# A Mamba block with a top-2 mixture of experts: the last chunk's output in two parts, and rows added in the result buffer

## The reference, cut to what matters

```python
xz = xn @ W_in                                   # 256 -> 2 x 512
u = silu(causal_conv4(xz[:, :512]) + conv_b)
dt, B, C = split(u @ W_xproj, [16, 32])          # 16, 16, 16
delta = softplus(dt @ W_dt + b_dt)
h[t] = exp(delta[t] * A) * h[t-1] + delta[t] * u[t] * B[t]     # 512 channels x 16 states
y[t] = sum_n h[t] * C[t] + D_skip * u[t]
mamba = (y * silu(z)) @ W_out                    # 512 -> 256
moe = sum over the top 2 of 16 experts: weight * (gelu(ln(xn @ W1 + b1)) @ W2 + b2)
```

## Time and profile before

| | us |
|---|---|
| median of 3 runs | 1177.31 |
| lowest and highest | 1170.78, 1178.3 |
| the profiled execution | 1172.21 |
| its span | 1170.5 |

### The profile page before, as it was taken

How to read it: one execution, slowest core, us unless ns; L and a number is a source line. 1 busy time by engine, 2 the same in 40 slices (tenths; PEclk the granted TensorE clock), 3 DMA queues, 4 the chain that set the end, 5 groups by cost and what they waited for, 6 DMA issues and landing times.

```text
span 1170.5 us, 16709 instructions
## 1 busy us (share of the span) xinstructions
PE 961.2 (82%) x4499; PEld 646.5 (55%) x4499; DVE 1051.2 (90%) x1310; ACT 863.6 (74%) x1787; POOL 839.3 (72%) x549
## 2 busy tenths in 40 slices
PE   5955576697979989789887998899988999778766
PEld 2423244464547656566555756476556665566655
DVE  7699959999999799989688969999899989979993
ACT  3444497655788788867798689978998699967860
POOL 8005488888678677558677786977987768877993
PEclk9966797588979989899998999799997999989886
DMA  9987865763366523834447542763457453854215
GB/s 320 406 355 228 260 199 152 243 231 95 105 223 194 123 65 80 317 101 97 105 118 258 150 101 68 261 205 66 102 151 245 114 121 74 285 167 106 71 18 171
DMA packets 129879, 197.52 MB, mean 169 GB/s; under 512 B 20924, under 2 KB 112744, under 8 KB 121464
## 3 DMA queue, kind: packets, MB, share of 16 engines
q1 hardware_dynamic: 105056, 156.73, 40.1%
q0 software_dynamic: 18288, 22.62, 11.5%
q10 hardware_dynamic: 6440, 17.10, 4.0%
HBM read 150.01 MB, written 54.20 MB: 174 GB/s over the span
## 4 chain that ended last, share of the span: by engine, by line
PE 36%; issue 18%; ACT 15%; DVE 15%; POOL 8%; DMA 3%; ACTq 2%; SPq 1%; POOLq 0%; DVEq 0%
DVE hb L1450 10%; PE psY L1002 7%; POOL hc L613 5%; PE psA L1027 5%; PE psC L1145 4%; ACT hb L774 4%; PE psC L1086 3%; PE psA L1074 3%; DVE psB L1439 3%; ACT hnT L860 2%; PE psE L1122 2%; PE psA L1019 2%; DMA xg<-xs_d 2%; POOL acc_d L653 1%; ACT L863 1%
## 5 line engine op out<-in xcount | busy, mean ns | idle before, releaser
L613 POOL TENSOR_TENSOR hc<-hb,Cb 128x1024 f32<-128x1024 f32 x235 | 597.0, 2612 | 127.3 <-PE psY L1002 70.6
L1450 DVE TENSOR_TENSOR_SCAN hb<-hb,carry,psB 128x512 f32<-128x512 f32 x384 | 471.6, 1264 | 1.4 <-ACT hb L774 1.4
L1002 PE MATMUL psY<-ident,hc 128*128 128x128 f32 x2048 | 315.6, 296 | 74.1 <-POOL hc L613 60.8
L1002 PEld LDWEIGHTS psY<-ident,hc 128*128 128x128 f32 x2048 | 263.6, 153 | 195.6 <-POOL hc L613 90.6
L774 ACT ACTIVATE hb<-delta,aneg 128x512 f32<-128x512 f32 x512 | 349.0, 717 | 15.2 <-DVE delta L1288 7.0
L1439 DVE TENSOR_TENSOR psB<-Bb,psU 128x512 f32<-128x512 f32 x512 | 325.5, 681 | 0.0
L653 POOL DMA_INDIRECT acc_d<-yo,idx x80 | 127.9, 1599 | 67.7 <-DMA acc_d<-yo,idx 23.0
L1450 DVE TENSOR_TENSOR_SCAN hb<-hb,psB 128x512 f32<-128x512 f32 x128 | 149.5, 1204 | 6.1 <-ACT hb L774 6.1
L1027 PE MATMUL psA<-ux,dgw 128*128 128x512 f32 x232 | 120.2, 628 | 11.6 <-ACT ux L718 11.4
L627 POOL DMA_INDIRECT xs_d<-xg,slots x64 | 66.9, 1045 | 50.5 <-issue 27.7
L1145 PE MATMUL psC<-w2r,hnT 128*128 128x256 f32 x320 | 89.1, 426 | 0.0
(11 more groups left out here) (211 smaller groups left out, 1198.1 us busy)
## 6 DMA issues: line engine op xcount, KB each, us to landing
Bb<-bc_d SPq DMA_DIRECT2D x32, 1024.0 KB, 6.4
...
Bb<-in_L_attn_x SPq DMA_DIRECT2D x8, 512.0 KB, 8.9
```

Of the source, the lines that this page charges most:

```text
L613: pool.tensor_tensor(hc[:, k:k + 2, :], hb[:, g % HR:g % HR + 2, :], Cb[:, n:n + 2, :], ALU.mult).then_inc(s_g, 1)
L1002: mm = pe.matmul(y[:, tt * P:(tt + 1) * P], hc[:, g % GR, tt * P:(tt + 1) * P], ident[:, :], start=False, stop=(n == NS - 1), is_transpose ...
L1450: dve.tensor_tensor_scan(h, h, psB[g % 2][:, :], first, ALU.mult, ALU.add).then_inc(s_scan, 1)
```

## The change

- Chunk 7's quarters 0 to 2 are transposed, projected and copied to `om` during the last units (`p_tr`, `p_trc`, `p_mm`, `p_copy`), and GpSimd adds them as an eighth chunk add at unit 509. Gate 2 of chunk 7 moves from unit 62 to 52. Behind the last gate one transpose per tile, two copies of 128 x 256 and four projections are left; VectorE adds them to the rows read back in two additions of 128 x 512, and SyncE stores two halves.
- All adds go to `out`, which now has the padding rows; the copy of 3584 rows is gone, and the host takes the middle 4096 rows.
- Pairs 176, 186, 200 and 414 leave `HC_DVE` and so go to GpSimd.
- `idx` moves by one unit, W1's centring (`CEN0`) by one, and some forty entries of the tables by one to a few units.

```diff
 AT = {
...
-    "gate": [30, 39, 52, 2],
+    "gate": [30, 39, 52, 3],
...
 AT7 = {
...
-    "gate": [37, 40, 63, 2],
+    "gate": [36, 40, 52, 3],
...
+    "p_tr": [53, 56, 57, 59],
+    "p_trc": [56, 58, 60, 60],
+    "p_mm": [53, 58, 59, 63],
+    "p_copy": [57, 59, 60, 60],
 }
...
-HC_DVE = [0, 2, 4, 6, 8, 10, 14, 16, 22, 38, 54, 72, 78, 86, 146, 176, 184, 186, 200, 398, 414]
+HC_DVE = [0, 2, 4, 6, 8, 10, 14, 16, 22, 38, 54, 72, 78, 86, 146, 184, 398]
...
-    "idx": [5],
+    "idx": [6],
...
-CEN0 = 5
+CEN0 = 6
...
-    return tiles + ([("chunk", c - 1, 0)] if c > 0 and s == AT["e_copy"][TT - 1] + 2 else [])
+    if c > 0 and s == AT["e_copy"][TT - 1] + 2:
+        tiles.append(("chunk", c - 1, 0))
+    if c == NC - 1 and s == AT7["p_copy"][TT - 1] + 1:
+        tiles.append(("chunk", c, 0))
+    return tiles
...
+        def dc_out(c):
+
+            return DC - 1 if c == NC - 1 else DC
...
         def acc_rows(c):
-            return acc_d[1 + c * T:1 + (c + 1) * T, :].rearrange("(a p) d -> p a d", p=P)
+            return out[1 + c * T:1 + (c + 1) * T, :].rearrange("(a p) d -> p a d", p=P)
...
             sp.dma_start(yo[:, :, :], acc_rows(NC - 1)).then_inc(s_fa, 16)
-            sp.dma_start(out[0:NT - T, :].rearrange("(p a) d -> p (a d)", p=P),
-                         acc_d[1:1 + NT - T, :].rearrange("(p a) d -> p (a d)", p=P)).then_inc(s_fo, 16)
-            for tt in range(TT):
-                r = (NC - 1) * T + tt * P
-                sp.wait_ge(s_eo, tt + 1)
-                sp.dma_start(out[r:r + P, :], om[:, tt, :]).then_inc(s_fo, 16)
-            sp.wait_ge(s_fo, 16 * (1 + TT))
+            for k in range(2):
+                sp.wait_ge(s_eo, k + 1)
+                sp.dma_start(acc_rows(NC - 1)[:, 2 * k:2 * k + 2, :], om[:, 2 * k:2 * k + 2, :]).then_inc(s_fo, 16)
+            sp.wait_ge(s_fo, 16 * 2)
...
+                    if c == NC - 1:
+                        for tt in range(TT):
+                            for _ in at(c, "p_trc", s, tt, tt + 1):
+                                y_copy(c, tt)
+                            for _ in at(c, "p_copy", s, tt, tt + 1):
+                                o_copy(c, tt)
...
+            act.wait_ge(s_ltm, 1)
+            act.wait_ge(s_eom, NC * TT)
+            for k in range(2):
+                act.activation(ygT[:, 2 * k:2 * k + 2, :], psC[:, 2 * k * P:2 * (k + 1) * P].rearrange("p (a b) -> p a b", a=2),
                                ACT.Copy).then_inc(s_et, 1)
...
+            pe.wait_ge(s_c, len(C_TURN))
             for tt in range(TT):
...
+                mm = pe.matmul(psC[:, tt * P:(tt + 1) * P], zs[:, tt, (DC - 1) * P:DC * P], ident[:, :],
+                               start=True, stop=True, is_transpose=True)
+            mm.then_inc(s_ltm, 1)
...
+            for k in range(2):
+                pe.wait_ge(s_et, k + 1)
+                for a in range(2):
+                    mm = pe.matmul((psE, psA)[k][:, a * D:(a + 1) * D], ygT[:, 2 * k + a, :], wout[:, DC - 1, :],
+                                   start=True, stop=True)
+                mm.then_inc(s_lom, 1)
...
-            for tt in range(TT):
-                dve.wait_ge(s_eom, (NC - 1) * TT + tt + 1)
-                dve.tensor_tensor(om[:, tt, :], (psC, psE)[tt % 2][:, 0:D], yo[:, tt, :], ALU.add).then_inc(s_eo, 1)
+            for k in range(2):
+                dve.wait_ge(s_lom, k + 1)
+                dve.tensor_tensor(om[:, 2 * k:2 * k + 2, :], (psE, psA)[k][:, :].rearrange("p (a d) -> p a d", a=2),
+                                  yo[:, 2 * k:2 * k + 2, :], ALU.add).then_inc(s_eo, 1)
```

More of the change, by code:

```diff
@@ L75 @@
 AT0 = {
-    "x_load": [31],
+    "x_load": [34],
     "x_mm": [7, 7, 11, 12, 12, 13, 18, 18, 21, 21, 22, 23, 26, 29, 32, 32, 33, 33, 33, 34, 36, 36, 37, 37],
-    "x_in": [8, 19, 28, 34],
-    "x_copy": [10, 21, 32, 38],
-    "x_silu": [38],
-    "xd_mm": [42, 42, 44, 44],
-    "xd_copy": [40],
-    "d_mm": [49, 55, 61, 7],
-    "d_exp": [46, 52, 60, 6],
-    "d_ln": [50, 59, 61, 2],
+    "x_in": [7, 15, 28, 32],
+    "x_copy": [10, 19, 32, 38],
+    "x_silu": [41],
+    "xd_mm": [41, 42, 44, 44],
+    "xd_copy": [46],
+    "d_mm": [49, 54, 61, 3],
+    "d_exp": [46, 54, 60, 3],
+    "d_ln": [50, 59, 60, 0],
     "d_max": [52, 58, 62, 5],
     "d0_exp": [2, 4, 6],
-    "d0_max": [3, 5, 9],
-    "du": [50, 6, 20, 29],
-    "z_mm": [14, 15, 25, 26],
-    "z_copy": [14, 14, 24, 25],
-    "z_silu": [29],
-    "gate": [30, 38, 57, 15],
+    "d0_max": [4, 5, 9],
+    "du": [50, 6, 23, 30],
+    "z_mm": [14, 14, 24, 25],
+    "z_copy": [14, 15, 24, 25],
+    "z_silu": [28],
+    "gate": [31, 38, 55, 16],
     "dskip": [3, 4, 36, 40],
     "bc_load": [48, 57, 61, 63],
-    "carry": [0],
+    "carry": [1],
 }
 AT7 = {
-    "d_mm": [42, 56, 57, 2],
-    "d_exp": [49, 49, 63, 5],
-    "d_ln": [35, 45, 58, 5],
-    "d_max": [49, 49, 62, 8],
-    "du": [53, 1, 13, 34],
-    "z_mm": [12, 13, 23, 28],
+    "d_mm": [43, 55, 60, 2],
+    "d_exp": [41, 50, 63, 5],
+    "d_ln": [33, 50, 61, 5],
+    "d_max": [47, 49, 62, 11],
+    "du": [52, 7, 15, 32],
+    "z_mm": [12, 15, 25, 29],
     "z_copy": [13, 20, 28, 30],
     "z_silu": [31],
-    "gate": [37, 40, 63, 2],
-    "dskip": [4, 10, 34, 47],
+    "gate": [36, 40, 52, 3],
+    "dskip": [4, 9, 34, 46],
     "carry": [0],
+    "p_tr": [53, 56, 57, 59],
+    "p_trc": [56, 58, 60, 60],
+    "p_mm": [53, 58, 59, 63],
+    "p_copy": [57, 59, 60, 60],
 }
-HC_DVE = [0, 2, 4, 6, 8, 10, 14, 16, 22, 38, 54, 72, 78, 86, 146, 176, 184, 186, 200, 398, 414]
+HC_DVE = [0, 2, 4, 6, 8, 10, 14, 16, 22, 38, 54, 72, 78, 86, 146, 184, 398]
 PUT0 = 7
@@ L120 @@
     "load": [0],
-    "load1": [0, 4],
+    "load1": [3, 4],
     "load2": [15],
@@ L181, in evictions_at @@
                            for kind, step in (("y", "e_trc"), ("o", "e_copy")) for _ in at(c, step, s, tt, tt + 1)]
+    e += [(kind, c, tt) for tt in range(TT)
+          for kind, step in (("y", "p_trc"), ("o", "p_copy")) if c == NC - 1 for _ in at(c, step, s, tt, tt + 1)]
     return e + [(kind, g, h) for g, off in groups_at(G) for h in range(GT // 2)
```

72 lines of the change are left out of this document (28 added, 44 removed).

## The result

| | before | after |
|---|---|---|
| median us | 1175.28 (20 runs) | 1181.57 (20 runs) |
| profiled execution, its span | 1172.21, 1170.5 | 1181.12, 1179.4 |

The ratio is 1.0062 with a 95% interval of 1.0046 to 1.0079: 0.0062 x 1175.28 = 7.3 us slower, where 0.9% faster was forecast. It leaves out one run of before that took 1227.42 us, and it is not the quotient of the medians, which lie 6.3 us apart. After's median of 1181.57 lies 0.6 us above the stated range of 1155 to 1181, and within 1% of no change, but on the other side of it.

The account below looks back on a forecast made before the run. VectorE's row of pairs plus its waits was taken as the bound. Terms -0.4 - 2.2 - 2.4 - 1.4 - 4.1 = -10.5 us took the profiled 1172.2 to 1161.7, stated as median 1166.5 us, range 1155 to 1181.

Parts of the forecast that it names:

- the multiplies: Chunks 2 and 6: four times-C multiplies move from VectorE to GpSimd; -0.4 us at pair 176, 0 at 186 and 200, -2.2 at 414.
- the index step: Chunk 4's start: one multiply passes ahead of GpSimd's index step, so TensorE's 2.37 us wait goes; -2.4 us.
- chunk 0's row loads: Chunk 0: a pair of loads now stands ahead of the load SyncE blocks on for 14.2 us; -1.4 us.
- the end: Behind the last scan: three of four channel quarters leave the stretch after the last gate, a wait is added; -4.1 us.
- the +2 for ScalarE's order in chunk 0: Chunk 0: unfavourable end of the row loads' term, since ScalarE's new order there is not in the trace; +2 us.
- the +0.7 for gate 2 of the last chunk: Last chunk: gate 2 is done ten units earlier, ahead of the last scans, and adds 0.7 us to them.
- GpSimd becomes the bound: Rival: moved multiplies meet GpSimd's waits for row adds and lie in the open; +11 us, 1188; chance 0.1.
- it passes them on: Chunk 4: TensorE, busy 57 of the next 60 us, carries its saved 2.37 us to the chunk's first gate; -2.4 us.
- one of the forecast's own signs of being wrong: Chunk 0: a gate wait changed by more than 3 us would show the forecast wrong.
- The added wait: End: GpSimd's chunk add waits for the row add and delays the last multiply from 1148.90 to 1153.5; +4.6 us.
- two projections at 3.78 / 8 = 0.47 each are 0.95: End: TensorE's time for each half behind the last gate, giving halves at 1161.9 and 1162.8.
- The rule that was weighed against the trace: End: the skill's estimate of 3.2 us for the chunk add, against 5.9 to 7.5 traced; sum 0.6 us lower.

Follow-up runs that it names:

- the ladder: Four kernels on one chip, each adding one more group of the change to before with the new end: 1.0003, 1.0021, 1.0046, 1.0040 of before.
- at_delta: Before with only the four new delta-chain rows of the table for chunks 1 to 7: 1.0044 of before.
- delta_back: After with the delta chain's entries in AT and AT0 put back as before: 0.9999 of before.
- ladder1: Before with the new end, the later index step and the table rows no run had tried, mostly chunk 7's: 1.0003 of before.
- ladder2: ladder1 with the new delta rows of chunks 1 to 7 as well: 1.0021 of before.
- ladder4: The changed kernel itself, the same as after, measured again on another chip: 1.0040 of before.
- hc_back: After with the old HC_DVE, so pairs 176, 186, 200 and 414 back on VectorE: 1.0041 of before.
- hc414: Before with only pair 414's multiply, in chunk 6, moved from VectorE to GpSimd: 0.9982 of before.

## Why the prediction was wrong

**The step that failed is one that isn't there.** The forecast summed four parts, the multiplies, the index step, chunk 0's row loads and the end. The "some forty entries of the tables" that move by one to a few units had no term; the sum gave them nothing, and the only bounds that touch them are the +2 for ScalarE's order in chunk 0 and the +0.7 for gate 2 of the last chunk. By the runs they are the largest part (as ratios): delta rows of chunks 1 to 7 +0.0044 alone and +0.0018 on the ladder, the rows untried until then +0.0042 (of which chunk 7's +0.0017 alone), chunk 0's with centring and `load1` +0.0025 on the ladder and +0.0009 alone. On the ladder that is 0.0085, 10 us, against the 10.5 that were to be gained. That after with the old delta rows is at 0.9999 says the same from the other side. The waits behind it are shown for chunk 7 (5.16 us between two gates where there were 0.71). For the delta rows only the cost is shown (`at_delta`, and `delta_back` against after), and where it arises stays open. My explanation was that a logarithm with one exp more ahead of it in ScalarE's queue makes VectorE's maximum wait, and the traces don't bear it out: with these rows alone the maxima wait 7.2 us in all (7.4 before), from ladder1 to ladder2 10.6 and 10.8, and without them in `delta_back` still 15.4. Another place is VectorE's own multiplies by C. Their time and the wait ahead of them together go from 48.0 us before to 50.3 in `at_delta`, from 44.2 in ladder1 to 49.2 in ladder2, and from 36.0 in `delta_back` to 45.0 in after. But ladder4, the same kernel as after, has 37.9, so single traces don't decide it. None of the rivals named the tables either. "GpSimd becomes the bound" had the sign, but with the four multiplies back on VectorE (`hc_back`) the kernel is still at 1.0041, and the added waits at maxima and scans in after's trace name ScalarE.

**The multiplies: right in size alone, within the noise.** Pair 414: -2.2 forecast, 0.9982 (-2.1) measured, and 57.5 us between its gates in `hc414` against 59.6. The three of chunk 2: -0.4 forecast, 0.9987 measured. In the changed kernel they gained next to nothing (1.0046 to 1.0040), which the forecast did not foresee. What it left out as well are the scans behind them, which now wait for ScalarE. In after:

```profile
544.87 2.45 DVE L1463 TENSOR_TENSOR_SCAN hb<-hb,carry,psB 128x512 f32<-128x512 f32 x2 [1.58 <-ACT hb L785]
...
551.16 1.28 DVE L1463 TENSOR_TENSOR_SCAN hb<-hb,carry,psB 128x512 f32<-128x512 f32 x1 [1.47 <-ACT hb L785]
...
994.44 1.28 DVE L1463 TENSOR_TENSOR_SCAN hb<-hb,carry,psB 128x512 f32<-128x512 f32 x1 [1.25 <-ACT carry L791]
```

The first two waits (1.58 or 1.59 and 1.47 us) stand in every trace with the three multiplies of chunk 2 moved, the third in every trace with 414 moved; where the multiplies stay, there is 0.30 us or nothing. So most of the 4.7 us more that the scans wait in after comes with the multiplies, and takes back much of the 4.9 us that they save.

**The index step: size right at the gate, -2.4 forecast and 4.48 - 1.93 = 2.55 measured.** The step "it passes them on" failed: alone the gate gained 3.4 us and the next maximum gave nearly all of it back; the ratio, 0.9986, leaves 1.6 us, and its trace leaves it 2.3 us ahead at the last gate by a shorter wait at the last gate of chunk 6, where two traces of one kernel differ by more than that.

**Chunk 0's row loads: -1.4 forecast, none seen.** Before, all four puts ahead of the multiply ran behind the wait of 12.10 us. In after three of them had run by 125, but the fourth waited 14.21 us and the multiply behind it started at 140.09 against 140.29. The step that failed is that SyncE's wait goes with its order: the 14.2 us for the store became 14.9 us for the landing of a put whose rows the next load overwrites.

```profile
SPq L455 <- DMA xs_d<-xg,slots: 15.5, 2, 14.9
```

The chunk's first gate came 0.36 us later than before and waited 6.12 us instead of 9.25, so VectorE itself reached it some 3.5 us later; a change of more than 3 us there was one of the forecast's own signs of being wrong. By the last gate of the chunk it was 3.1 us late.

**The end: -4.1 forecast, 0.9975 or -2.9 measured, -2.6 in after's trace.** The added wait was right: +4.6 forecast, 4.46 measured. From gate to span end I had 7.9 us, and it took 9.45. The mis-sized term is "two projections at 3.78 / 8 = 0.47 each are 0.95": the 8 records in the earlier trace rows are two for each projection, so two of them take 1.9 us a half (2.05 and 1.91). That makes TensorE 0.95 and 1.9 us later than I had it, so it, and not the read back as forecast, had the last word: the first closing addition waited for psE. The rule that was weighed against the trace did no better. In after a chunk add took 6.2 to 8.0 us from issue to landing; the Trainium skill (DMA: Bandwidth & Descriptors, "Anatomy of one DMA — SWDGE (gpsimd) path") gives an estimate of 3.2 us for its 512 KB, and the trace disagrees again.
